# A two-layer perceiver kernel on one core: other queues, another order and unread products before its first score step

## The reference

```python
x = x + L0_xattn(layernorm(x), ctx)      # x @ W1.T + mean over the 1601 ctx rows @ W2.T + b
x = x + L0_attn(layernorm(x))            # 16 heads over 64 rows, slopes[h] * distance added to the scores
x = x + L0_ffn(layernorm(x))             # shared MLP, and 8 experts, two chosen for each row
x = x + L1_xattn(layernorm(x), ctx)      # 16 heads of 16; keys and values: 1601 rows of ctx @ Wk.T, @ Wv.T
x = x + L1_attn(layernorm(x))            # causal convolution, gated recurrence, MLP
x = x + L1_ffn(layernorm(x))             # quantized MLP 256 -> 1024 -> 256
```

## Time and profile before

| what | before |
|---|---|
| median of 3 runs | 2175.66 us |
| the profiled execution | 2174.97 us, span 2173.2 us |
| TensorE busy | 1977.2 us, 91% |
| VectorE, ScalarE, GpSimd busy | 61%, 48%, 28% |
| TensorE's mean granted clock | 0.982 |

### The profile page before, as it was taken

How to read it: one execution, slowest core, us unless ns; L and a number is a source line. 1 busy time by engine, 2 the same in 40 slices (tenths; PEclk the granted TensorE clock), 3 DMA queues, 4 the chain that set the end, 5 groups by cost and what they waited for, 6 DMA issues and landing times.

```text
span 2173.2 us, 72578 instructions
## 1 busy us (share of the span) xinstructions
PE 1977.2 (91%) x31813; PEld 1596.8 (73%) x31813; DVE 1328.9 (61%) x2495; ACT 1049.6 (48%) x1534; POOL 613.0 (28%) x998
## 2 busy tenths in 40 slices
PE   4788989999999999999999999999999988999887
PEld 4567777777877777777777777777777777777764
DVE  2456755856666567656656676665666666565534
ACT  2344545554455555545555555554544444434432
POOL 3222332323233232333323223332323222122201
PEclk8899999999999999999999999999999999999999
DMA  4343423433423343334233424243342321222122
GB/s 160 140 150 109 142 87 125 149 125 124 139 88 114 116 141 129 130 107 151 83 125 109 171 77 138 92 150 106 110 148 89 116 79 31 89 83 81 48 66 72
DMA packets 99255, 243.91 MB, mean 112 GB/s; under 512 B 13312, under 2 KB 19584, under 8 KB 98944
## 3 DMA queue, kind: packets, MB, share of 16 engines
q1 hardware_dynamic: 98944, 239.26, 32.5%
HBM read 235.94 MB, written 3.15 MB: 110 GB/s over the span
## 4 chain that ended last, share of the span: by engine, by line
PE 71%; DVE 14%; ACT 9%; issue 4%; SPq 1%; POOL 1%; DMA 1%; DVEq 0%; POOLq 0%; ACTq 0%
PE M L780 12%; PE SC L977 9%; PE M L787 9%; PE SC L1000 8%; PE O L1021 7%; ACT probT L1220 6%; PE X L827 5%; DVE mx L1559 4%; PE SC L993 3%; PE M L827 3%; PE X L1101 2%; PE M L868 2%; DVE oT L1571 1%; PE X L1088 1%; PE M L832 1%
## 5 line engine op out<-in xcount | busy, mean ns | idle before, releaser
L1559 DVE TENSOR_REDUCE mx<-SC 128x4 f32<-128x1600 f32 (+1 forms) x256 | 466.5, 1822 | 131.4 <-PE SC L977 128.2
L1220 ACT ACTIVATE probT<-SC 128x2048 f32<-128x2048 f32 (+1 forms) x256 | 398.8, 1558 | 227.2 <-PE SC L1000 226.5
L634 POOL TENSOR_TENSOR rowsT<-raw,rowsT 128x384 fp32r<-128x384 f32 (+1 forms) x256 | 277.8, 1106 | 405.0 <-ACT rowsT L1278 404.9
L787 PE MATMUL M<-wvs,rowsT 128*128 128x256 f32 x2496 | 358.3, 292 | 3.2 <-issue 1.6
L780 PE MATMUL M<-rowsT,wks 128*128 128x400 f32 (+1 forms) x1536 | 334.5, 363 | 12.0 <-DVE V L1362 7.6
L780 PEld LDWEIGHTS M<-rowsT,wks 128*128 128x128 f32 x1536 | 276.2, 192 | 84.5 <-issue 61.5
L1362 DVE TENSOR_TENSOR V<-M,bv 128x256 f32<-128x256 f32 (+1 forms) x448 | 159.6, 398 | 287.4 <-PE M L787 276.6
L787 PEld LDWEIGHTS M<-wvs,rowsT 128*128 128x128 f32 x2496 | 314.8, 192 | 23.5 <-issue 3.5
L1165 ACT ACTIVATE kT<-M,bk 128x400 f32<-128x400 f32 (+1 forms) x256 | 151.6, 594 | 350.6 <-PE M L780 350.2
L977 PE MATMUL SC<-kT,bdq 32*128 32x400 f32 (+1 forms) x2048 | 248.1, 553 | 49.9 <-ACT probT L1220 42.7
L1021 PEld LDWEIGHTS O<-probT,V 128*17 128x17 f32 x13312 | 191.3, 98 | 72.2 <-issue 66.6
(11 more groups left out here) (266 smaller groups left out, 2464.1 us busy)
## 6 DMA issues: line engine op xcount, KB each, us to landing
ring<-in_ws_dram SPq DMA_DIRECT2D x428, 256.0 KB, 4.5
raw<-in_ctx_dram SPq DMA_DIRECT2D x32, 1601.0 KB, 8.4
summed<-in_ctx_dram SPq DMA_DIRECT2D x60, 800.5 KB, 4.5
ring<-rounded_scratch SPq DMA_DIRECT2D x64, 256.0 KB, 5.4
out_dram<-x SPq DMA_DIRECT2D x16, 128.0 KB, 3.2
kT<-in_ctx_dram SPq DMA_DIRECT2D x2, 800.5 KB, 8.9
x<-in_x_dram SPq DMA_DIRECT2D x11, 128.0 KB, 2.0
rounded_scratch<-wround SPq DMA_DIRECT2D x8, 128.0 KB, 2.2
```

The costliest lines, as they stand in the source:

```text
L634: pool.tensor_tensor(rowsT[1][:, c, at], raw[:, c, at], rowsT[0][:, c, at], ALU.subtract).then_inc(low_ready, 1)
L787: mm = pe.matmul(bank[:, (t - 2 * a) * D:(t - 2 * a + 1) * D], rowsT[xp][:, cc, t * P:(t + 1) * P], wvs[wp][:, cc, :], start=(at == cc == ...
L1220: act.activation(probT[step % 3][0:w, :, 0:len(ts), :].rearrange("p j t q -> p j (t q)"), SC[0:w, :, 0:len(ts) * P], ACT.Exp)\
L1559: dve.tensor_reduce(mx[c][:, :, n], SC[:, :, 0:KCH[n][1]], AX.X, ALU.max).then_inc(max_used, 1)
```

## The change

- The transfers of bq0, bk0, dist, the slopes, wkv, bv0, bo0 and wg are issued from ScalarE's stream at its start, before it preloads its table of exponentials; wkv counts on a semaphore of its own (`wkv_in`). SyncE keeps the five of `in_`, in another order, and the first users of these wait for 80 instead of 112.
- Of the sums for batch 1, VectorE makes the second half; ScalarE makes the first and the means, later in its slot. `prepare` moves ahead of VectorE's sums.
- `high_weights` and GpSimd's `clear` move to slot -25, `low_weights` from -17 to -20; the splits of batch 0 start five slots earlier on ScalarE (-24, -24, -20, -19) and follow on GpSimd at -20, -20, -19, -18. Before, ScalarE's were at -19, -18, -17, -16.
- `EARLY` starts at -20 with value(0), and puts the keys ahead of most values.
- Sixteen unread products of 512 columns stand before the first `l0_xa`, and five before each of the maxima of steps 1 to 4. They write bank X.
- In the tail, `IDLE['xq']` goes from 5 to 15 and `busy_rows` goes.

```diff
@@ -92,7 +92,7 @@
-IDLE = {'sums': 2, 'out': 9, 'conv_in': 4, 'pw': 10, 'gru_in': 7, 'hg0': 2, 'hg1': 3, 'gow': 10, 'ff_in': 7, 'ff0': 2, 'fow': 0, 'xq': 5, 'up0': 0, 'hq': 14, 'down': 4}
+IDLE = {'sums': 2, 'out': 9, 'conv_in': 4, 'pw': 10, 'gru_in': 7, 'hg0': 2, 'hg1': 3, 'gow': 10, 'ff_in': 7, 'ff0': 2, 'fow': 0, 'xq': 15, 'up0': 0, 'hq': 14, 'down': 4}
@@ -146,9 +146,12 @@
-EARLY = {-16: [key(0, 0), key(0, 1)], -15: [key(0, 2), key(0, 3)], -14: [value(0), value(1), value(2)], -13: [value(3), value(4)], -12: [value(5)], -11: [key(1, 0)], -10: [key(1, 1)], -9: [key(1, 2)], -8: [key(1, 3)], -3: [value(6)]}
+EARLY = {-20: [value(0)], -18: [value(1)], -17: [key(0, 0), key(0, 1), key(0, 2)], -16: [key(0, 3), key(1, 0)], -15: [key(1, 1)], -12: [value(2), value(3)], -9: [key(1, 2)], -8: [key(1, 3)], -7: [value(4)], -6: [value(5)], -3: [value(6)]}
...
+FIRST_WARM = (1, 2, 3, 4)
 OWN = value(4), value(5), value(6)
-FIRST_SPLITS = (-19, -18, -17, -16)
...
+FIRST_SPLITS = (-24, -24, -20, -19), (-20, -20, -19, -18)
@@ -304,7 +307,7 @@
             yield n + 1, piece
-        if g == FIRST_SPLITS[piece]:
+        if STEPS * b + k == FIRST_SPLITS[late][piece]:
@@ -552,19 +556,9 @@
                     issued += 1
-                for t, src in ((bv0, d["l0bv"].partition_broadcast(P)), (bo0, d["l0bo"].partition_broadcast(P)), (wg, d["l0wg"]),
-                               (bq0, d["l0bq"]), (bk0, d["l0bk"]), (dist, d["dist"])):
-                    whole(t, src, early_in)
-                head_pairs = d["slopes"].rearrange("(j a) -> a j", a=2)
-                for n in range(2):
-                    sync.dma_start(slopes[n * S:(n + 1) * S, :], head_pairs[n].partition_broadcast(S),
-                                   allow_slow_non_contiguous=True).then_inc(early_in, 16)
-                for t, src in ((wk, d["wkv"][:, 0, :, :]), (wv, d["wkv"][:, 1, :, :])):
-                    sync.dma_start(t, src).then_inc(in_, 16)
-                for t, src in ((bk, d["l1bk"]), (perm, d["perm"]), (bq, d["l1bq"])):
+                sync.dma_start(bvv[:, :, :].rearrange("p h f -> p (h f)"), d["l1bv"].partition_broadcast(P)).then_inc(in_, 16)
+                for t, src in ((bk, d["l1bk"]), (bq, d["l1bq"]), (bo, d["l1bo"].partition_broadcast(P)), (perm, d["perm"])):
                     whole(t, src, in_)
-                sync.dma_start(bvv[:, :, :].rearrange("p h f -> p (h f)"), d["l1bv"].partition_broadcast(P)).then_inc(in_, 16)
-                whole(bo, d["l1bo"].partition_broadcast(P), in_)
@@ -730,14 +724,14 @@
                         split_max(b + 1, 0)
-                    if g == L0_START[0] + 5:
+                    if g == L0_START[0] + 2:
...
                         if t == 0 and k == 0:
-                            pool.wait_ge(in_, 112)
+                            pool.wait_ge(in_, 80)
@@ -749,7 +743,7 @@
                         layer0(i, q)
-                    if g == L0_START[0] + 1:
+                    if g == FIRST_CYCLE:
@@ -833,6 +827,9 @@
                 def layer0(what, i, kind, f, bank):
+                    if (i, kind) == (0, "l0_xa"):
+                        pe.wait_ge(cleared, 1)
+                        warm(16)
@@ -959,12 +956,20 @@
+                def warm(count):
...
+                    for _ in range(count):
+                        pe.matmul(X.rearrange("p (a t) -> p a t", a=4), identb[:, :], identb[:, :].unsqueeze(1).to_broadcast([P, 4, P]),
+                                  start=True, stop=True, skip_group_check=True)
...
                     k0, kn = KCH[n]
+                    if s in FIRST_WARM:
+                        warm(5)
@@ -1036,23 +1041,11 @@
-                def busy_rows(columns_):
...
-                    for wp, xp in PARTS:
-                        for j in range(4):
-                            r = slice(32 * j, 32 * j + 32)
-                            pe.matmul(SC[:, j, 0:columns_], rowsT[wp][r, 0, 0:P], rowsT[xp][r, 1, 0:columns_], start=True, stop=True, skip_group_check=True)
...
                         busy(IDLE.get(kind, 0))
-                        if kind == "xq":
-                            busy_rows(400)
-                            busy_rows(400)
-                            busy_rows(128)
-                            busy_rows(128)
@@ -1116,7 +1109,6 @@
                     if STEPS * b + k == min(EARLY):
-                        pe.wait_ge(in_, 112)
@@ -1143,6 +1135,18 @@
+                for t, src in ((bq0, d["l0bq"]), (bk0, d["l0bk"]), (dist, d["dist"])):
+                    act.dma_start(full(t), src).then_inc(early_in, 16)
+                head_pairs = d["slopes"].rearrange("(j a) -> a j", a=2)
+                for n in range(2):
+                    act.dma_start(slopes[n * S:(n + 1) * S, :], head_pairs[n].partition_broadcast(S),
+                                  allow_slow_non_contiguous=True).then_inc(early_in, 16)
+                for t, src in ((wk, d["wkv"][:, 0, :, :]), (wv, d["wkv"][:, 1, :, :])):
+                    act.dma_start(t, src).then_inc(wkv_in, 16)
+                for t, src in ((bv0, d["l0bv"].partition_broadcast(P)), (bo0, d["l0bo"].partition_broadcast(P)), (wg, d["l0wg"])):
+                    act.dma_start(full(t), src).then_inc(early_in, 16)
+                act.preload_act_table(ACT.Exp)
@@ -1162,6 +1166,8 @@
                         k0, kn = KCH[a]
+                        if what == (0, *key(0, 0)):
+                            act.wait_ge(in_, 80)
@@ -1278,7 +1284,7 @@
                 def high_weights():
-                    act.wait_ge(in_, 112)
+                    act.wait_ge(wkv_in, 32)
@@ -1290,7 +1296,9 @@
                         src = summed[:, :]
-                    act.activation(src, src, ACT.Copy, accum_out=msum[:, j % 2, c:c + 1]).then_inc(sum_added, 1)
...
+                    if (j, c) != (1, 1):
+                        act.activation(src, src, ACT.Copy, accum_out=msum[:, j % 2, c:c + 1]).then_inc(sum_added, 1)
@@ -1307,7 +1315,7 @@
                     load_table(b, k, ACT.Gelu)
-                    if STEPS * b + k == L0_START[0] + 5:
+                    if STEPS * b + k == FIRST_CYCLE:
@@ -1323,12 +1331,16 @@
                     for j, c in sums(b, k):
-                        context_sum(j, c)
+                        if j > 1:
+                            context_sum(j, c)
...
                             drain(what)
+                    for j, c in sums(b, k):
+                        if j == 1:
+                            context_sum(j, c)
@@ -1355,6 +1367,8 @@
                         m = min(2 * a + 2, KT) - 2 * a
+                        if what == (0, *value(0)):
+                            dve.wait_ge(in_, 80)
@@ -1731,7 +1745,7 @@
                 def clear():
-                    dve.wait_ge(in_, 112)
+                    dve.wait_ge(in_, 80)
@@ -1744,10 +1758,11 @@
                         if (i, q) == (0, 1):
+                            prepare()
...
                             dve.tensor_reduce(msum[:, 0, :], raw[:, :, 0:KEYS], AX.X, ALU.add).then_inc(fast_sum, 1)
-                        if (i, q) == (0, 3):
-                            prepare()
+                            dve.wait_ge(batch_landed, 32)
+                            dve.tensor_reduce(msum[:, 1, 1:2], kT[1][:, 0:KEYS], AX.X, ALU.add).then_inc(sum_added, 1)
```

1 line of the change is left out of this document (added).

## The result

The changed kernel takes 2199.33 us (median of 4 runs, 2196.44 to 2203.22), the kernel before 2174.42 (4 runs, 2171.54 to 2180.36): ratio 1.0112, 95% interval 1.0085 to 1.0140, or 24.9 us slower. The forecast was 2167.5 us with a range up to 2179. The profiled execution took 2196.44 us (span 2194.6), 21.5 more than the one of before.

What follows compares the result with a forecast made beforehand. TensorE was taken as the bound from 120 to 2118 us, so only earlier time could move; 7.4 - 12.0 - 2.0 - 1.5 = -8.1 us gave 2167.5 us (-0.37%), with an 8-in-10 range of 2157 to 2179 us.

Steps and rivals of the forecast that it cites:

- The first wait: Start of the kernel up to TensorE's l0_xa: it would start near 25.5 us instead of 18.1, +7.4 us.
- E: Landing time of the last small input: taken as 16 us, with bounds 8.85 and 29.04.
- the first route: Before l0_xa: GpSimd's lower weight halves, then sixteen unread products on TensorE, would let l0_xa start at 25.0 us.
- Rival D: First wait: the slopes' 4-byte packets hold up ScalarE's queue, l0_xa at 38.6 us; total +5.5 us, 2181 us; chance 0.12.
- slower by 0.5% needs E past 30: Whole kernel: a slowdown over 0.5% requires the last small input to land after 30 us; chance 0.06.
- The chain to the first maxima: From l0_xa to the first maxima, 60.5 us before: -12.0 us, bounds -17 and -7.
- From the PT turns to the output product: From the first PT turn to L899: value products moved out from between, -7.5 us.
- from there to the maxima: From L899 to the first maxima: more value and fewer key products +1.3 us, a fall of the clock +2.3.
- From the maxima to step 0: From the first maxima to step 0: faster products if the clock stays up, less 2 us for unread ones; net -2 us.
- Behind step 0: From 103 to 120 us, where TensorE's clock was 0.52: -1.5 us, between 0 and -5.
- From there an earlier start should reach the end one for one: From the first score step on: time gained before it would be kept whole to the end.
- The tail: End of the kernel: forty-eight products of L1044 give way to ten more of the bf16 form, 0 us.

Runs made afterwards that it cites:

- e5: The changed kernel with the slopes as 128 rows of 32 bytes and without the 36 unread products: ratio 1.0025 to the kernel before.
- e13: The changed kernel, its 4-byte slopes kept, without the 36 unread products: ratio 1.0067 to the kernel before.
- e1: The changed kernel with the slopes brought as 128 rows of 32 bytes instead of 1024 packets of 4 bytes: ratio 1.0080 to the kernel before.
- e10: e9 with the table of the first keys and values (`EARLY`) as in the kernel before: ratio 0.9972 to the kernel before.
- e7: The kernel before with the slopes as rows of 32 bytes and 36 unread products of 4 columns in the first wait: ratio 1.0024 to the kernel before.
- e9: e5 with `prepare()` put back behind the third piece of layer 0: ratio 0.9983 to the kernel before.
- e3: The changed kernel with its ten ScalarE transfers issued by SyncE again, the new order kept on all engines: ratio 1.0118 to the kernel before.

## Why the prediction was wrong

**The first wait** was sized at +7.4 and measured +22.1 us. The route was right: VectorE, behind `prepare()`, decides. The step that failed is the landing E of the last small input, taken at 16 by the nearest row, xab; it was 29.9. The same packets put the first route late too: GpSimd's lower halves, reckoned done at 19.1 us, were done at 30.3, because wkv, whose copies start at 26.58, stood behind them as well. Rival D had both the place and the cause, the 4-byte packets holding up ScalarE's queue, with 38.6 us for l0_xa where 40.23 came. It got 0.12 because I set three small transfers against all that SyncE had moved by 18.10 us, and counted bytes. The queue was to be counted in packets: 1024 from the slopes, each with one of SyncE's beside it. The upper end of E was no bound either (29.04, its time as before), and `prepare()` took 4.4 us instead of 3.8, for it now runs beside GpSimd's low parts. Rival D had the total wrong all the same, +5.5 us where 24.9 came. The sentence that slower by 0.5% needs E past 30 doesn't come out of the prediction's own terms: with 15 us gained behind l0_xa it would need E past 34, and E at 29.9 would give +6.4.

**The chain to the first maxima** was -12.0 and is -5.8. From the PT turns to the output product -6.9 (forecast -7.5), from there to the maxima +2.7 (forecast +3.6 with the clock's fall), from L865 to the turns +0.3 (forecast -1.2): in order. From l0_xa to L865 it is -1.9 instead of -6.9: to the turn of n0 -0.3 (forecast -1.7), from there to the v products -0.8 (-1.8), and from these to L865 -0.7 (-3.4). `prepare()` is out of ScalarE's way as I said (its eviction starts 3.2 us behind the start of the q and k products, 7.1 before). The middle step is short because the clock did not stay up: the q and k products took 3.17 us, where 1.95 was reckoned. In the other two, the values that left the PT turns had to go somewhere: 2.77 us of them stand between l0_xa and the turn of n0, 1.69 between k and L865, each with VectorE's eviction behind it (0.94 us idle at 55.33). I had named these 24 products as "done before" and had not asked before what.

**From the maxima to step 0** -2 was forecast and -2.3 came, and the clock was 0.98 in this stretch (94.91 to 117.11 us), 0.71 before. The number is right by luck. The gain was put down to a clock that stays up, less 2 us for the four groups of unread products. But e5 and e13 have none of these products and take 21.2 us for the same stretch, 1.0 less than with them (22.2 in e1 and in the changed kernel), at a clock of 0.92 and 0.93; e10, with the old order, takes 23.5. So the new order gives the gain, and the unread products take a part of it. **Behind step 0** the forecast had 1.5 us from a clock that falls less. In the first 17 us it is what it was (103.07 us on in before, 117.11 on in after):

```profile
103.07:120.07 17.00, 10.90 (x105) 7.95 (x104) 9.41 (x10) 7.22 (x7) 6.06 (x6) 0.52 0.31 111
...
117.11:134.11 17.00, 10.90 (x103) 7.95 (x104) 9.45 (x10) 7.21 (x7) 5.00 (x5) 0.52 0.32 111
```

**"From there an earlier start should reach the end one for one"** is the second step that failed: -1.5 forecast, +7.4 in the profiled pair, +12 to +17 in the other kernels with a shift of 36 or 72 instructions, and by the ratios of e5, e7 and e13 10 to 12 us. I took the stretch behind step 0 as untouched because the change puts nothing into it; but 36 products more ahead of it move every later instruction against the ends of the 16 KB packets, where TensorE can stand still. None of my rivals had this.

**The tail**: 57.3 us from the last exponential's record to the end in before, 58.7 after; e1, e5, e9 and e10, with the same tail as the changed kernel, have 57.2 or 57.3. So 0, as forecast.

By the ratios, taken off one after another: the slopes' packets 7 us (1.0112 to 1.0080), the unread products 12 (to 1.0025; 10 by e13), `prepare()` ahead of the sums 9 (to 0.9983), the new order 2 (to 0.9972), which can't be told from nothing. The intervals of two such ratios are as wide as the smaller of these steps. These are 30 us of loss against the 24.9 measured; the 6 between them are what the rest gains, and that is no more than the kernel before has with the slopes mended (0.9977).

## What to carry to other kernels

Count a queue in packets before it shares the DMA engines with a stream that matters: each of a thousand 4-byte packets took a turn from the other queue here, and that queue fell from 883 to 348 packets in 4 us. Before work is moved ahead of a wait, ask what the engines put in front of it wait for themselves. And where one engine with tens of thousands of instructions is the bound, adding a few at its start is no local edit: compare the stalls put down to issue behind the edit, and try a few paddings in a free wait; here 92 cheap products went with 12 us (0.9972 to 0.9916) against the same kernel without them, some 8 of them at equal granted clock. Such a gain holds for one order of instructions only: any later edit ahead of it moves the places again.

## What the hardware showed that I had not expected

- Two queues with work are served packet for packet: 716 against 714 in 10 us, though the one's packets hold 2.9 KB on average and the other's 4 bytes; what the DMA engines moved went from 301 to 220 GB/s over the first 18.10 us.
- TensorE stands still for 1.0 to 2.5 us at places that come back when 256 instructions are added ahead of them, and goes on 1.18 to 1.68 us after the end of a 16 KB instruction packet (91 of 92 stalls). Four such stalls stand in the kernel before, thirteen in the worst kernels here.
- The same six VectorE instructions of `prepare()` took 1.1 us with GpSimd idle (e3), 3.8 and 4.4 beside GpSimd's low parts (before, after).
- An fp32 product of 4 columns on a 128x128 weight takes 0.213 us for each of its two records (27.31 us for 128), a bf16 one 0.03 us (2.64 us for 92).
- Sixteen unread products of 512 columns took 5.57 to 6.46 us, between the two levels of the clock. The next four records ran at the upper one in the changed kernel, 4.25 us later (1.10 us, 2.08 before), and at the lower one in e1, 3.36 us later (2.04); and the changed kernel's q and k products, 7 us later and behind a wait, took 3.17 us against 1.95 at the full clock.
